# Turning v on VectorE and scaling the attention heads on GpSimd, in an attention and mixture-of-experts layer on one core

## Chip, cores and metric

The kernel runs on one NeuronCore of one Trainium2 chip. The metric is the device time of one execution in microseconds (us). The engines are named as the profile names them: PE (TensorE matmul), PEld (its weight loads), DVE (VectorE), ACT (ScalarE), POOL (GpSimd) and SP (SyncE, which here only issues DMAs). Each engine runs its own instructions in the order in which they were written; they meet through semaphores.

## What is computed

One layer in float32: layer norm, attention with rotary positions, a band mask and a sink column, an output projection and a residual; then layer norm again and a mixture of 8 experts with 2 chosen per token. Cut to what the change touches:

```python
# x: (4, 512, 256); NQ = 32 query heads, NKV = 8 key/value heads, HD = 64
proj = layernorm(x) @ W_qkv
q, k, v = split(proj)
q, k = rope(q), rope(k)
attn = where(mask, -inf, q @ k.T / sqrt(HD))
w = softmax(concat([attn, sink]))[..., :-1]
x = x + (w @ v).reshape(B, L, NQ * HD) @ W_out
x = x + moe(layernorm(x))
```

## The kernel before

**Groups and periods.** The attention part works through 32 groups, 8 key/value heads times 4 batches. A group has one k, one v and four query heads. Its scores come in 16 units of 128x512, two at a time from one PE step. One group's scores take one period; a period has 16 steps, and in each step every engine is given, in this order, work of the group whose scores run (step n of `*_step`), of the next group (n - 16), of the one before (n + 16) and of the one before that (n + 32), and last work of the router. The tables of numbers (`PROJ_PAIR_AT`, `ROT_AT`, `HEADS_AT` and so on) say at which n a piece is written. There is no scheduler: the order on an engine is the order of writing.

**A group's way through the engines.** PE projects k, v and the first two query heads in two halves (`project_pair`, L1508), in steps 0 and 2 of the period before the group's own. ACT copies them out (`chunk_out`, L844) into `chunk_sb`: the tile named KV has k in partitions 0 to 63 and v in 64 to 127; Q01 and Q23 hold two query heads each. For the rotation, SP moves halves of these tiles into `swap_sb` by DMA (`swap_halves`, L492), and POOL rotates (`rotate`, L691, L692 and L696, three instructions per tile; KV's have 64 partitions). The rotated k is doubled by a DMA (`k_twice`). The first score of a group (L1562, n = 0) waits for the rotated KV and Q01 of its group.

**v.** PE turns v by four transposes into a PSUM bank (`turn_v`, L1526, written ahead of the last third of the probabilities times v), ACT copies it to `v_next` (L852), SP stores it to `v_rows` in DRAM (L505) and reads it back four times into `v_quads` (L513), for four 32-row quadrants.

**Probabilities and heads.** DVE takes each unit's scores out of PSUM with the mask and the row maximum (L1162), ACT takes the exponent (L862), DVE turns two units at a time in 32x32 blocks (L1171). In the next period PE multiplies them with v into four PSUM banks `PV` (L1586: 80, 80 and 96 instructions in steps 4, 6 and 8). The denominators go POOL (`sink_arg` L709, `denom` L719), DVE (reciprocal L1180, transpose L1184, after the second unit of the next group), then SP: to DRAM (L521) and back, spread over all partitions, into `recip_wide` (L529). DVE scales the four banks into `heads_sb` (L1191) in step 9. PE projects the heads (L1618, steps 12 and 14), ACT copies the result out (L869, L872, L876), and POOL adds it to the residual (L726, two instructions).

**POOL's and SP's order in a period.** POOL: split of the next weights (L648, L657), rotate Q23, rotate KV, rotate Q01 (step 5), the two residual additions (step 6); with steps 15 and 16 of the group, `sink_arg` and `denom`. In some periods of batches 1 to 3, DMAs with a scatter index are issued from POOL for the router (L774), two of them in step 9. SP: `recip_out`, `recip_spread`, the KV swaps, the Q01 swaps, `k_twice`, three loads of weights, the store and the four loads of v, the Q23 swaps.

Of the kernel before, what the change touches and what calls it, by code (L numbers as in the profile page):

```python
# [20 lines left out]
F32 = mybir.dt.float32  # L21
# [5 lines left out]
P = 128  # L27
# [3 lines left out]
TPB = L // P  # L31
# [28 lines left out]
def moe_layer(nc, x, w_qkv, w_out, sink, gate_w, w1, b1, w2, b2, rope, out):  # L60
    ctx = ExitStack()
    with ctx:
        slot_rows = nc.dram_tensor("slot_rows", (E * CAP, ROW), F32, kind="Internal").ap()

        v_rows = nc.dram_tensor("v_rows", (P, TPB * HD), F32, kind="Internal").ap()
# [111 lines left out]
        s_v_next = sem("s_v_next")  # L177
# [8 lines left out]
        s_heads = sem("s_heads")  # L186
        s_y = sem("s_y")
# [73 lines left out]
        v_next = sb("v_next", [P, TPB, HD], c=actx)  # L261
        qk_st.append(sb("qk_st1", [P, PAIRS + 1, L], c=actx))
        v_quads = [sb(f"v_quads{i}", [P, TPB, TPB * HD], c=actx) for i in range(2)]
# [13 lines left out]
        xn1 = v_next[:, :, :].rearrange("p t d -> p (t d)")  # L277
# [63 lines left out]
        TURN_V_AT, V_NEXT_AT = -8, -7  # L341
        ROT_AT = {2: Q23, -12: KV, -11: Q01}
# [9 lines left out]
        Y_FIRST_OUT_AT, Y_OUT_AT, RESIDUAL_AT = 30, 31, 38  # L352
        ODD_ORDER = (1, 0)
# [85 lines left out]
        def turned_v_bank(g):  # L439

            return PV[0] if g == 0 else PROJ

# [24 lines left out]
        def _(sp):  # L467
# [32 lines left out]
            def v_out(g):  # L500

                sp.wait_ge(s_v_next, g + 1)
                if g > 0:
                    sp.wait_ge(s_v_in[(g - 1) % 2], ((g - 1) // 2 + 1) * (16 * QUADS))
                sp.dma_start(v_rows, v_next[:, :, :].rearrange("p t d -> p (t d)")).then_inc(s_v_out, 16)  # L505

            def v_in(g, j):

                sp.wait_ge(s_v_out, g * 16 + 16)
# [114 lines left out]
        def _(pool):  # L624
# [75 lines left out]
            def pool_step(n, g, j):  # L700
# [19 lines left out]
                if n == RESIDUAL_AT and g < GROUPS - 1:  # L720
                    for i, odd in enumerate(ODD_ORDER):
                        pool.wait_ge(s_y_out, 2 * g + i + 1)
                        if later(2 * g + i):
                            pool.wait_ge(s_residual, 2 * g + i)
                        t = (g // NKV) * TPB + odd
                        nc.gpsimd.tensor_tensor(x_sb[:, t:t + 3:2, :], x_sb[:, t:t + 3:2, :], y_sb[odd][:, :, :],  # L726
                                                ALU.add).then_inc(s_residual, 1)
# [92 lines left out]
        def _(act):  # L820
# [16 lines left out]
            def chunk_out(g, c):  # L837
# [4 lines left out]
                if c == Q23 and g > 0:  # L842
                    act.wait_ge(s_v_turned, g + 1)
# [4 lines left out]
            def v_copy(g):  # L848
                act.wait_ge(s_v_turned, g + 1)
                if g > 0:  # L850
                    act.wait_ge(s_v_out, g * 16)
                nc.scalar.activation(v_next[:, :, :], turned_v_bank(g)[:, 0:TPB * HD].rearrange("p (c d) -> p c d", d=HD),  # L852
                                     ACT.Copy).then_inc(s_v_next, 1)

            def act_step(n, g, j):
                if n in CHUNK_OUT_AT:
                    chunk_out(g, CHUNK_OUT_AT[n])
                if n == V_NEXT_AT:
                    v_copy(g)
                if 0 <= n < UNITS:  # L860
# [3 lines left out]
                                         accum_out=sums[j][:, n:n + 1]).then_inc(s_probs, 1)  # L864
                if n == Y_FIRST_OUT_AT and g < GROUPS - 1:
# [50 lines left out]
            v_copy(0)  # L916
# [44 lines left out]
            def act_ahead(m):  # L961
# [28 lines left out]
                if m in LATE_NORM_AT:  # L990
                    i = LATE_NORM_AT[m]
                    act.wait_ge(s_late, 1 if i < TPB else 2)
                    act.wait_ge(s_v_out, (LATE_PERIODS[i] + 1) * 16)
                    nc.scalar.activation(xn1, x_sb[:, TPB + i, :], ACT.Identity,
# [111 lines left out]
        def _(dve):  # L1106
# [49 lines left out]

            def dve_step(n, g, j):
# [27 lines left out]
                if n == HEADS_AT:  # L1185
                    dve.wait_ge(s_pv, g + 1 + 1)
                    dve.wait_ge(s_recip_in, g * 32 + 32)
                    if later(2 * g):
                        dve.wait_ge(s_y, 2 * g + 1)
# [186 lines left out]
            rotate_q()  # L1376
            dve.wait_ge(s_mask, 1)
# [87 lines left out]
        def _(pe):  # L1465
# [16 lines left out]
            def project(g, j, c):  # L1482
# [4 lines left out]
                else:  # L1487
                    pe.wait_ge(s_v_next, g + 1)
# [25 lines left out]

            def turn_v(g):
                pe.wait_ge(s_chunk_out, g * CHUNKS + (Q01 if g > 0 else KV) + 1)
                if g % NKV == 3 and g > NKV:
                    pe.wait_ge(s_x2T, 2 * (g // NKV))
                if g % NKV == 4 and g > NKV:
                    pe.wait_ge(s_centred, g // NKV)  # L1520
                if g % NKV == 5 and g > NKV:
                    pe.wait_ge(s_place, g // NKV)
                if g - 1 in LATE_PERIODS:
                    pe.wait_ge(s_xT_lo, TPB + LATE_PERIODS.index(g - 1) + 1)
# [23 lines left out]
            def pe_step(n, g, j):  # L1548
# [15 lines left out]
                if n in PV_AT:  # L1564
# [16 lines left out]
                    for blk in PV_AT[n]:  # L1581
                        c, d = divmod(blk, TPB)
                        for a in range(QUADS):
                            rows = slice(a * BLK, (a + 1) * BLK)
                            for p in range(PAIRS):
                                ins = nc.tensor.matmul(PV[a][p * HD:(p + 1) * HD, 0:2 * P],  # L1586
                                                       v_quads[j][rows, d, c * HD:(c + 1) * HD],
# [38 lines left out]
                if n == TURN_V_AT:  # L1626
                    turn_v(g)
# [173 lines left out]
```

## Time and profile before

| | |
|---|---|
| median of 3 runs | 1054.57 us (1053.58 to 1058.2) |
| the profiled execution | 1057.24 us, of which its span is 1055.5 us |
| mean granted TensorE clock, share of full speed | 0.993 |
| busy, share of the span | PE 97%, DVE 88%, POOL 63%, ACT 62% |
| DMA | 112.10 MB in 155893 packets |
| chain that ended last, by engine | PE 56%, DVE 37%, issue 3% |
| chain, largest lines | PE L1586 22%, DVE L1162 16%, DVE L1171 14%, PE L1562 10%, DVE L1191 4% |

Times inside the trace are counted from the first instruction. The attention part ends at about 800 us and the experts follow. The chain of work that ended last is followed back from the last instruction, at each step to what released it. An engine's idle time is given with what released the instruction after it; "issue" there means that nothing which the profile shows was waited for.

### The profile page before, as it was taken

To read this page: it belongs to the slowest core of one execution; us is meant where nothing else is said; L and a number is where in the kernel's file an instruction comes from. 1 tells how busy PE (TensorE), PEld (TensorE's weight loads), DVE (VectorE), ACT (ScalarE), POOL (GpSimd) and SP (SyncE) were. 2 spreads that over 40 slices of the span, in tenths; PEclk is the share of its full clock that TensorE was granted. 3 is DMA by queue.
4 is the path that set the end of the run, shared out by engine and by line. 5 is a ranking of instruction groups with operands and counts; after the bars stand their busy time and mean duration, and the time that the engine had idled before them with its cause. 6 is when DMAs were issued, how large, how long until landed. Compare 5 with 4: busy or idle time off the path is not lost.

```text
span 1055.5 us, 32277 instructions
## 1 busy us (share of the span) xinstructions
PE 1024.9 (97%) x12943; PEld 720.9 (68%) x12943; DVE 926.8 (88%) x1967; ACT 655.0 (62%) x1671; POOL 665.1 (63%) x607
## 2 busy tenths in 40 slices
PE   7899999999999999999999999999988999999996
PEld 4466666666666666666666666666656999999995
DVE  6999999999999999999999999999985787777773
ACT  4666667666667766667776666776663555445551
POOL 6667776777666888666787777777752333333332
PEclk9999999999999999999999999999989999999998
DMA  3534544544333334333334334333424555555521
GB/s 112 142 108 118 137 131 140 132 112 135 93 83 83 96 99 111 99 104 81 80 95 114 100 103 121 98 83 96 119 70 162 119 119 123 117 123 124 101 46 21
DMA packets 155893, 112.10 MB, mean 106 GB/s; under 512 B 76480, under 2 KB 145152, under 8 KB 155616
## 3 DMA queue, kind: packets, MB, share of 16 engines
q1 hardware_dynamic: 137680, 90.03, 33.0%
q0 software_dynamic: 7296, 8.55, 4.8%
q10 hardware_dynamic: 10768, 11.46, 3.6%
q8 instruction: 102, 1.67, 0.7%
q14 instruction: 47, 0.39, 0.1%
HBM read 74.84 MB, written 21.83 MB: 92 GB/s over the span
## 4 chain that ended last, share of the span: by engine, by line
PE 56%; DVE 37%; issue 3%; ACT 1%; POOL 1%; DMA 1%; SPq 0%; POOLq 0%; DVEq 0%; ACTq 0%
PE bank L1586 22%; DVE probs_ring L1162 16%; DVE probs_t L1171 14%; PE bank L1562 10%; PE bank L1739 9%; PE bank L1750 6%; DVE heads_sb L1191 4%; PE bank L1753 3%; PE bank L1618 1%; PE bank L1508 1%; PE bank L1526 1%; PE bank L1533 1%; DVE neg_max L1162 0%; ACT probs_ring L862 0%; PE bank L1491 0%
## 5 line engine op out<-in xcount | busy, mean ns | idle before, releaser
L862 ACT ACTIVATE probs_ring<-probs_ring,neg_max 128x512 f32<-128x512 f32 x512 | 365.8, 717 | 210.3 <-DVE neg_max L1162 209.6
L1162 DVE CUSTOM_DVE_ANT_0 probs_ring<-bank,mask,sink_neg 128x512 f32<-128x512 f32 x512 | 360.1, 737 | 26.6 <-PE bank L1562 25.5
L1171 DVE STREAM_TRANSPOSE probs_t<-probs_ring 128x1024 f32<-128x1024 f32 x256 | 317.5, 1240 | 0.2 <-ACT probs_ring L862 0.2
L1562 PE MATMUL bank<-qk_st 64*128 64x512 f32 x1024 | 281.1, 625 | 11.9 <-DVE neg_max L1162 7.4
L1586 PE MATMUL bank<-probs_t,v_quads 32*64 32x256 f32 x8192 | 247.6, 381 | 0.1
L1586 PEld LDWEIGHTS bank<-probs_t,v_quads 32*64 32x64 f32 x8192 | 179.1, 132 | 76.5 <-issue 48.8
L691 POOL TENSOR_TENSOR chunk_sb<-chunk_sb,rope_sb 128x512 f32<-128x512 f32 (+1 forms) x94 | 120.0, 1276 | 103.9 <-issue 82.7
L810 POOL DMA_INDIRECT out<-expert_sb,slots x40 | 78.8, 1969 | 143.1 <-DVE expert_sb L1428 134.5
L1562 PEld LDWEIGHTS bank<-qk_st 64*128 64x128 f32 x1024 | 85.3, 186 | 77.4 <-DVE neg_max L1162 41.8
L696 POOL TENSOR_TENSOR qk_st<-chunk_sb,swap_sb 128x512 f32<-128x512 f32 (+1 forms) x94 | 120.2, 1279 | 7.4
L1618 PEld LDWEIGHTS bank<-wo_sb,heads_sb 64*128 64x128 f32 x992 | 96.1, 187 | 37.4 <-issue 29.2
L692 POOL TENSOR_TENSOR swap_sb<-swap_sb,rope_sb 128x512 f32<-128x512 f32 (+1 forms) x94 | 120.5, 1281 | 0.0
L1077 ACT ACTIVATE hidden<-bank,b_sb 128x320 f32<-128x320 f32 x128 | 60.6, 525 | 95.7 <-PE bank L1739 95.7
L1618 PE MATMUL bank<-wo_sb,heads_sb 64*128 64x256 f32 x992 | 117.4, 376 | 0.0
L1750 PE MATMUL bank<-w_part,hidden_hi 128*128 128x512 f32 x320 | 114.1, 398 | 0.0
L1508 PE MATMUL bank<-xcur,w_hi 64*128 64x512 f32 x496 | 100.9, 481 | 0.0
L862 ACT ACTIVATION_READ_ACCUMULATOR probs_ring<-probs_ring,neg_max 128x1 f32 x512 | 97.4, 190 | 0.0
L1753 PE MATMUL bank<-w_part,hidden_lo 128*128 128x256 f32 x320 | 90.1, 282 | 0.0
L726 POOL TENSOR_TENSOR x_sb<-x_sb,y_sb 128x512 f32<-128x512 f32 x62 | 79.2, 1277 | 4.5
L1739 PE MATMUL bank<-slots_hi,w_hi 128*128 128x320 f32 x256 | 79.5, 310 | 0.5 <-DVE expert_sb L1428 0.5
L1739 PE MATMUL bank<-slots_lo,w_hi 128*128 128x320 f32 x256 | 79.0, 308 | 0.0
L1739 PE MATMUL bank<-slots_hi,w_lo 128*128 128x320 f32 x256 | 79.0, 308 | 0.0
(191 smaller groups left out, 1342.7 us busy)
## 6 DMA issues: line engine op xcount, KB each, us to landing
v_quads<-v_rows SPq DMA_DIRECT2D x128, 128.0 KB
recip_wide<-recip_rows SPq DMA_DIRECT2D x64, 256.0 KB
w_raw<-in_L_ffn_w SPq DMA_DIRECT2D x14, 1024.0 KB, 7.6
swap_sb<-chunk_sb SPq DMA_DIRECT2D x314, 32.0 KB
w_raw<-in_L_attn_W_qkv SPq DMA_DIRECT2D x32, 256.0 KB, 2.9
slot_rows<-x2T ACTq DMA_DIRECT2D x8, 662.5 KB, 5.8
slots_cut<-slot_rows SPq DMA_DIRECT2D x56, 80.0 KB, 3.0
w_raw<-in_L_attn_W_qkv SPq DMA_DIRECT2D x64, 64.0 KB, 2.7
```

The source lines that it names most:

```text
L691: nc.gpsimd.tensor_tensor(straight, straight, rope_sb[rows, 0, :], ALU.mult).then_inc(s_pool, 1)
L692: nc.gpsimd.tensor_tensor(swapped, swapped, rope_sb[rows, 1, :], ALU.mult).then_inc(s_pool, 1)
L696: nc.gpsimd.tensor_tensor(qk_st[j][rows, PAIRS if c == KV else c - Q01, :], straight, swapped, ALU.add).then_inc(s_rot, 1)
L862: nc.scalar.activation(probs[(g * UNITS + n) % RING][:, :], probs[(g * UNITS + n) % RING][:, :], ACT.Exp, bias=neg_max[j][:, n:n + 1], sca ...
L1162: nc.vector.tensor_tensor_reduce(probs[(g * UNITS + n) % RING][:, :], SCORE[SCORE_OF[n // 2][n % 2]][:, :], mask[:, L - P - t * P:2 * L - ...
L1171: nc.vector.transpose(probs_t[j][:, :, (h // 2) * (2 * P):(h // 2 + 1) * (2 * P)] .rearrange("p b (h q) -> p h b q", h=2)[:, :, :, t * BLK ...
L1562: nc.tensor.matmul(SCORE[SCORE_OF[n // 2][hh]][:, :], qk_st[j][half, h // 2, t * P:(t + 1) * P], qk_st[j][half, PAIRS, :], start=True, sto ...
L1586: ins = nc.tensor.matmul(PV[a][p * HD:(p + 1) * HD, 0:2 * P], v_quads[j][rows, d, c * HD:(c + 1) * HD], probs_t[j][rows, blk, p * 2 * P:(p ...
L1618: ins = nc.tensor.matmul(PV[a][:, 0:D], heads_sb[rows, a, h * P:(h + 1) * P], wo_sb[rows, (g % NKV) * 2 + h, :], start=(half == 0 and h == ...
L1739: ins = nc.tensor.matmul(banks[4 + 2 * (c % 2) + half][:, 0:HALF], w[:, kc, c * P:(c + 1) * P], a[:, at:at + HALF], start=(kc == 0 and m = ...
L1750: nc.tensor.matmul(FFN2[s][:, :], hidden_hi[:, c, s * P:(s + 1) * P], w2_parts[e % 2][:, c, :, :].rearrange("p t d -> p (t d)"), start=(c ...
L1753: ins = nc.tensor.matmul(FFN2[s][:, 0:D], hidden_lo[:, c, s * P:(s + 1) * P], w2_hi[e % 2][:, c, :], start=False, stop=(c == HC - 1))
```

## The change

v is no longer turned by PE. DVE turns it with one transpose in 32x32 blocks (`turn_v`, step 9, where the scaling of the heads was), out of the KV tile into partitions 64 to 127 of the KV swap tile, which were free. The ACT copy to `v_next` is gone. SP stores the turned v with two DMAs whose runs are 128 B (before: one DMA with runs of 1 KB), and reads it back with runs of 4 KB (before: 1 KB). PE's waits that stood in `turn_v` move to the projection of Q23 (L1491), which follows two steps later.

The heads of all groups but the last are copied out of `PV` by ACT (four 128x256 copies, step 9) and scaled in place by POOL (two 128x512 multiplications, step 9), each half with a semaphore of its own; the output projection waits for the first half, and inside its first step for the second. The last group keeps DVE's scaling.

The late layer norms of later batches, which shared a buffer with `v_next`, get one of their own (`xn1`) and wait for PE's turning of the tile before instead of the store of v.

POOL's order changes: the rotation of Q01 moves from step 5 to step 10, behind the heads; the two residual additions move from one place in step 6 to steps 4 and 9.

```diff
-        TURN_V_AT, V_NEXT_AT = -8, -7
-        ROT_AT = {2: Q23, -12: KV, -11: Q01}
+        TURN_V_AT = -7
+        ROT_AT = {2: Q23, -12: KV, -6: Q01}
...
-        Y_FIRST_OUT_AT, Y_OUT_AT, RESIDUAL_AT = 30, 31, 38
-        ODD_ORDER = (1, 0)
+        Y_FIRST_OUT_AT, Y_OUT_AT = 30, 31
+        RESIDUAL_AT = {36: 1, 41: 0}
...
             def v_out(g):
-                sp.wait_ge(s_v_next, g + 1)
+                sp.wait_ge(s_v_turned, g + 1)
...
-                sp.dma_start(v_rows, v_next[:, :, :].rearrange("p t d -> p (t d)")).then_inc(s_v_out, 16)
+                for q in range(HD // BLK):
+                    sp.dma_start(v_rows.rearrange("j (b d) -> j b d", d=HD)[:, :, q * BLK:(q + 1) * BLK],
+                                 v_turned[q * BLK:(q + 1) * BLK, :].rearrange("j (b i) -> j b i", i=BLK)
+                                 ).then_inc(s_v_out, 16)
...
                 for a in range(QUADS):
-                    sp.dma_start(v_quads[j][a * BLK:(a + 1) * BLK, :, :],
-                                 v_rows.rearrange("(c j) n -> j c n", j=BLK)).then_inc(s_v_in[j], 16)
+                    sp.dma_start(v_quads[j][a * BLK:(a + 1) * BLK, :, :].rearrange("j b d -> j (b d)"),
+                                 v_rows).then_inc(s_v_in[j], 16)
...
+                if n == HEADS_AT and g < GROUPS - 1:
+                    pool.wait_ge(s_recip_in, g * 32 + 32)
+                    for half in range(2):
+                        part = slice(2 * half, 2 * half + 2)
+                        pool.wait_ge(s_heads_raw, 2 * g + half + 1)
+                        nc.gpsimd.tensor_tensor(heads_sb[:, part, :], heads_sb[:, part, :], recip_wide[:, part, :],
+                                                ALU.mult).then_inc(s_heads, 1)
...
+                if n == HEADS_AT and g < GROUPS - 1:
+                    act.wait_ge(s_pv, g + 1 + 1)
+                    if later(2 * g):
+                        act.wait_ge(s_y, 2 * g + 1)
+                    for a in range(QUADS):
+                        ins = nc.scalar.activation(heads_sb[:, a, :], PV[a][:, 0:2 * P], ACT.Copy)
+                        if a % 2 == 1:
+                            ins.then_inc(s_heads_raw, 1)
...
+            def turn_v(g):
+                dve.wait_ge(s_chunk_out, g * CHUNKS + KV + 1)
+                if g > 0:
+                    dve.wait_ge(s_v_out, g * 32)
+                nc.vector.transpose(v_turned, chunk_sb[KV][HD:P, :]).then_inc(s_v_turned, 1)
...
-                if n == HEADS_AT:
+                if n == TURN_V_AT and g > 0:
+                    turn_v(g)
+                if n == HEADS_AT and g == GROUPS - 1:
...
-                for c in range(TPB):
-                    ins = nc.tensor.transpose(turned_v_bank(g)[:, c * HD:(c + 1) * HD],
-                                              chunk_sb[KV][HD:P, c * P:(c + 1) * P],
-                                              identity[HD:P, HD:P])
-                ins.then_inc(s_v_turned, 1)
...
-                    pe.wait_ge(s_heads, 2 * g + (half if g == GROUPS - 1 else 1) + 1 + 1)
+                    pe.wait_ge(s_heads, 2 * g + half + 1 + 1)
...
+                            if half == 0 and second == 1:
+                                pe.wait_ge(s_heads, 2 * g + 1 + 1 + 1)
```

On POOL, in the period of group 13, one of those with two scatter DMAs in step 9, before: the last five rows of the rotations, the residual, the DMAs, and `sink_arg` and `denom` of the group.

```order
L691 TENSOR_TENSOR chunk_sb<-chunk_sb,rope_sb 64x512
L692 TENSOR_TENSOR swap_sb<-swap_sb,rope_sb 64x512
L696 TENSOR_TENSOR qk_st<-chunk_sb,swap_sb 64x512
L691 TENSOR_TENSOR chunk_sb<-chunk_sb,rope_sb 128x512
L692 TENSOR_TENSOR swap_sb<-swap_sb,rope_sb 128x512
L696 TENSOR_TENSOR qk_st<-chunk_sb,swap_sb 128x512
L726 TENSOR_TENSOR x_sb<-x_sb,y_sb 128x2x256 x2
L774 DMA slot_rows<-xn,scatter_idx 5120x265 x2
L709 TENSOR_TENSOR sink_arg<-neg_max,sink_neg 128x16
L719 TENSOR_TENSOR denom<-sums,sink_exp 128x16
```

The same place after; line numbers have moved by a few (L690, L691, L695 are the rotation, L733 the residual, L724 the heads, L781 the scatter).

```order
L690 TENSOR_TENSOR chunk_sb<-chunk_sb,rope_sb 64x512
L691 TENSOR_TENSOR swap_sb<-swap_sb,rope_sb 64x512
L695 TENSOR_TENSOR qk_st<-chunk_sb,swap_sb 64x512
L733 TENSOR_TENSOR x_sb<-x_sb,y_sb 128x2x256
L724 TENSOR_TENSOR heads_sb<-heads_sb,recip_wide 128x512 x2
L733 TENSOR_TENSOR x_sb<-x_sb,y_sb 128x2x256
L781 DMA slot_rows<-xn,scatter_idx 5120x265 x2
L690 TENSOR_TENSOR chunk_sb<-chunk_sb,rope_sb 128x512
L691 TENSOR_TENSOR swap_sb<-swap_sb,rope_sb 128x512
L695 TENSOR_TENSOR qk_st<-chunk_sb,swap_sb 128x512
L708 TENSOR_TENSOR sink_arg<-neg_max,sink_neg 128x16
L718 TENSOR_TENSOR denom<-sums,sink_exp 128x16
```

Between the rotation of KV (64 partitions) and that of Q01 (128) now stand a residual addition, both heads, the other residual addition and the scatter DMAs.

On DVE, around step 9 of a period in the middle of the attention part, before:

```order
L1171 STREAM_TRANSPOSE probs_t<-probs_ring 128x2x16x32
L1191 TENSOR_TENSOR heads_sb<-bank,recip_wide 128x256 x4
L1162 ISA probs_ring,neg_max<-bank,mask,sink_neg 128x512
L1162 ISA neg_max 128x1
L1162 ISA probs_ring,neg_max<-bank,mask,sink_neg 128x512
```

and after (L1174 takes the scores out, L1183 turns the probabilities):

```order
L1183 STREAM_TRANSPOSE probs_t<-probs_ring 128x2x16x32
L1167 STREAM_TRANSPOSE swap_sb<-chunk_sb 64x512
L1174 ISA probs_ring,neg_max<-bank,mask,sink_neg 128x512
L1174 ISA neg_max 128x1
L1174 ISA probs_ring,neg_max<-bank,mask,sink_neg 128x512
```

The four scaling instructions, which wait for the probabilities times v, give way to one transpose, which waits for the copied KV tile and for the store of the turned v of the group before.

## Rows read from the trace of the kernel before

**Rows 1.** Page, part 1: busy us (share of the span) xinstructions.

```profile
PE 1024.9 (97%) x12943; PEld 720.9 (68%) x12943; DVE 926.8 (88%) x1967; ACT 655.0 (62%) x1671; POOL 665.1 (63%) x607
```

**Rows 2.** DVE in time order: start us, us, what [idle before <-releaser].

```profile
417.44 1.42 DVE L1191 TENSOR_TENSOR heads_sb<-bank,recip_wide 128x256 f32<-128x256 f32 x4 [0.51 <-PE bank L1586]
418.78 0.74 DVE L1162 CUSTOM_DVE_ANT_0 probs_ring<-bank,mask,sink_neg 128x512 f32<-128x512 f32 x1
```

**Rows 3.** PE in time order, one period, first score to the next one's.

```profile
401.28 1.02 PE L1562 MATMUL bank<-qk_st 64*128 64x512 f32 x4
...
414.15 0.40 PE L1526 MATMUL bank<-identity,chunk_sb 64*128 64x64 f32 x4
414.49 2.85 PE L1586 MATMUL bank<-probs_t,v_quads 32*64 32x256 f32 x96
417.26 1.13 PE L1562 MATMUL bank<-qk_st 64*128 64x512 f32 x4
...
425.19 1.02 PE L1562 MATMUL bank<-qk_st 64*128 64x512 f32 x4
```

**Rows 4.** POOL in order of time, the same period.

```profile
412.83 1.27 POOL L691 TENSOR_TENSOR chunk_sb<-chunk_sb,rope_sb 64x512 f32<-64x512 f32 x1 [2.36 <-issue]
...
419.25 1.29 POOL L696 TENSOR_TENSOR qk_st<-chunk_sb,swap_sb 128x512 f32<-128x512 f32 x1
420.49 2.71 POOL L726 TENSOR_TENSOR x_sb<-x_sb,y_sb 128x512 f32<-128x512 f32 x2
```

**Rows 5.** Groups by line: xcount | busy us, mean ns | idle before.

```profile
L726 POOL TENSOR_TENSOR x_sb<-x_sb,y_sb 128x512 f32<-128x512 f32 x62 | 79.2, 1277 | 4.5
L691 POOL TENSOR_TENSOR chunk_sb<-chunk_sb,rope_sb 64x512 f32<-64x512 f32 x31 | 39.4, 1272 | 88.1 <-issue 82.7 <-DMA swap_sb<-chunk_sb 5.2
L774 POOL DMA_INDIRECT slot_rows<-xn,scatter_idx x32 | 32.4, 1013 | 39.4 <-DMA swap_sb<-chunk_sb 16.5 <-DVE xn L403 11.8 <-issue 6.0
L876 ACT ACTIVATE y_sb<-bank 128x256 f32<-128x256 f32 x62 | 20.2, 382 | 0.0
L1448 DVE STREAM_TRANSPOSE slots_t<-slots_cut 128x1280 f32<-128x1280 f32 x7 | 10.5, 1507 | 1.7 <-DMA slots_cut<-slot_rows 1.7
```

**Rows 6.** SP's issues in order of time, the period of rows 3.

```profile
406.79 1.29 SPq L529 DMA_DIRECT2D recip_wide<-recip_rows  x2
408.13 4.42 SPq L492 DMA_DIRECT2D swap_sb<-chunk_sb  x6
```

**Rows 7.** PE in time order: first scores of groups 1, 30 and 31.

```profile
41.07 1.09 PE L1562 MATMUL bank<-qk_st 64*128 64x512 f32 x3 [1.05 <-DVE neg_max L1162]
...
739.37 1.02 PE L1562 MATMUL bank<-qk_st 64*128 64x512 f32 x4
...
762.90 1.02 PE L1562 MATMUL bank<-qk_st 64*128 64x512 f32 x4
```

**Rows 8.** POOL in time order: KV's rotation begins, periods of groups 1 and 30.

```profile
54.96 1.28 POOL L691 TENSOR_TENSOR chunk_sb<-chunk_sb,rope_sb 64x512 f32<-64x512 f32 x1 [5.36 <-issue]
...
752.13 1.27 POOL L691 TENSOR_TENSOR chunk_sb<-chunk_sb,rope_sb 64x512 f32<-64x512 f32 x1
```

**Rows 9.** POOL in order of time: the second scatter DMA of a pair.

```profile
354.22 1.01 POOL L774 DMA_INDIRECT slot_rows<-xn,scatter_idx  x1 [0.30 <-issue]
```

**Rows 10.** POOL in order of time, period of group 31.

```profile
780.58 4.56 POOL L780 TENSOR_TENSOR w_lo<-w_raw,w_hi 128x2048 fp32r<-128x2048 f32 x1
789.12 0.22 POOL L709 TENSOR_TENSOR sink_arg<-neg_max,sink_neg 128x16 f32<-128x16 f32 x1 [3.98 <-DVE neg_max L1162]
```

**Rows 11.** A stretch: us, busy PE PEld DVE ACT POOL, clock, DMA, GB/s.

```profile
766.80:770.20 3.40, 2.58 (x20) 0.92 (x28) 3.06 (x7) 3.40 (x10) 2.72 (x3) 0.50 0.11 28
```

**Rows 12.** PE in order of time: scores in that stretch.

```profile
767.62 2.08 PE L1562 MATMUL bank<-qk_st 64*128 64x512 f32 x4 [1.72 <-DVE neg_max L1162]
```

**Rows 13.** DMA issues by line: xcount, KB each, median us from issue to landing.

```profile
slots_cut<-slot_rows SPq DMA_DIRECT2D x56, 80.0 KB, 3.0
v_rows<-v_next SPq DMA_DIRECT2D x32, 128.0 KB, 2.5
```

More of the change, by code:

```diff
@@ L260, in moe_layer @@
         y_sb = [sb(f"y_sb{i}", [P, 2, D], c=actx) for i in range(2)]
-        v_next = sb("v_next", [P, TPB, HD], c=actx)
+        xn1 = sb("xn1", [P, D], c=actx)
         qk_st.append(sb("qk_st1", [P, PAIRS + 1, L], c=actx))
-        v_quads = [sb(f"v_quads{i}", [P, TPB, TPB * HD], c=actx) for i in range(2)]
+        v_quads = [sb(f"v_quads{i}", [P, BLOCKS, HD], c=actx) for i in range(2)]
         probs_ring = sb("probs_ring", [P, RING, L], c=actx)
@@ L719, in pool_step @@
                     nc.gpsimd.tensor_tensor(denom[:, :], sums[j][:, :], sink_exp[:, :], ALU.add).then_inc(s_denom, 1)
[L720 to L727, printed above, removed]
+                if n == HEADS_AT and g < GROUPS - 1:
[5 more added lines that the diff above has]
+                                                ALU.mult).then_inc(s_heads, 1)
+                if n in RESIDUAL_AT and g < GROUPS - 1:
+                    odd = RESIDUAL_AT[n]
+                    i = 1 - odd
+                    pool.wait_ge(s_y_out, 2 * g + i + 1)
+                    if later(2 * g + i):
+                        pool.wait_ge(s_residual, 2 * g + i)
+                    t = (g // NKV) * TPB + odd
+                    nc.gpsimd.tensor_tensor(x_sb[:, t:t + 3:2, :], x_sb[:, t:t + 3:2, :], y_sb[odd][:, :, :],
+                                            ALU.add).then_inc(s_residual, 1)
             roots = [0]
@@ L841, in chunk_out @@
                     act.wait_ge(s_rot, q - CHUNKS + 1)
-                if c == Q23 and g > 0:
-                    act.wait_ge(s_v_turned, g + 1)
+                if c == KV and g > 0:
+                    act.wait_ge(s_v_turned, g)
                 nc.scalar.activation(chunk_sb[c][:, :].rearrange("p (c a i) -> p a c i", a=QUADS, i=BLK),
@@ L915, in _ @@
             chunk_out(0, Q23)
-            v_copy(0)
             def load_x(b):
@@ L992, in act_ahead @@
                     act.wait_ge(s_late, 1 if i < TPB else 2)
-                    act.wait_ge(s_v_out, (LATE_PERIODS[i] + 1) * 16)
-                    nc.scalar.activation(xn1, x_sb[:, TPB + i, :], ACT.Identity,
+                    if i > 0:
+                        act.wait_ge(s_norm_turned, TPB + i)
+                    nc.scalar.activation(xn1[:, :], x_sb[:, TPB + i, :], ACT.Identity,
                                          bias=bias_late[:, i:i + 1], scale=rstd_late[:, i:i + 1]).then_inc(s_norm, 1)
@@ L1376, in _ @@
             rotate_q()
+            turn_v(0)
             dve.wait_ge(s_mask, 1)
@@ L1487, in project @@
                 else:
-                    pe.wait_ge(s_v_next, g + 1)
+                    pe.wait_ge(s_chunk_out, g * CHUNKS + Q01 + 1)
+                    if g % NKV == 3 and g > NKV:
+                        pe.wait_ge(s_x2T, 2 * (g // NKV))
+                    if g % NKV == 4 and g > NKV:
+                        pe.wait_ge(s_centred, g // NKV)
+                    if g % NKV == 5 and g > NKV:
+                        pe.wait_ge(s_place, g // NKV)
+                    if g - 1 in LATE_PERIODS:
+                        pe.wait_ge(s_xT_lo, TPB + LATE_PERIODS.index(g - 1) + 1)
                 for kc in range(KC):
@@ L1639, in _ @@
             ins.then_inc(s_gate_cols, 1)
-            turn_v(0)
             SLOT_PIECES = [(0, 0, 4), (0, 4, 5), (1, 0, 3), (1, 3, 5)]
```

37 lines of the change are left out of this document (6 added, 31 removed).

## The prediction

> **What bounds the kernel now.** I read the engines' busy times first [rows 1]: PE 97% and DVE 88% leave little room, POOL stands at 63% and looks free. Then the chain of work that ended last: 56% PE and 37% DVE, hardly anything of POOL or DMA. In one period of the attention part the two take turns. PE runs the last third of the probabilities times v until 414.49 + 2.85 = 417.34 us [rows 3]; DVE sat idle 0.51 us for it and then scaled the heads in 1.42 us, and only at 418.78 did it take the next scores out of PSUM [rows 2], whose matmuls had been issued at 417.26 [rows 3]. So both things that the change takes off, PE's transposes and DVE's scaling, lie on the path that sets the end today.
>
> A 63% that is an average says nothing of when POOL must be done. PE may not issue the first score of a group before POOL has rotated its KV and Q01. In the period shown, POOL sat idle 2.36 us, began with KV at 412.83, and ended with Q01 at 419.25 + 1.29 = 420.54 [rows 4], 4.65 us before that score at 425.19 [rows 3]. POOL could not begin earlier: KV's group has 88.1 us of idle time before 31 instructions [rows 5], and what the code waits for there are the KV swaps, which SP issues behind the spread of the reciprocals [rows 6]. These wait in turn for the first scores of the running group. **KV's rotation therefore hangs on the first score of its period**, 412.83 - 401.28 = 11.55 us behind it here [rows 3, 4]. Over the periods of groups 1 to 30 (30 such pairs) the distance averages 12.34 us; the first is 54.96 - 41.07 = 13.89, the last 752.13 - 739.37 = 12.76 [rows 7, 8]. The mean period is (762.90 - 41.07) / 30 = 24.06 us [rows 7].
>
> **What goes from PE and DVE.** The next scores were issued at 417.26 and such a pair takes 1.13 us [rows 3]; without PE's transposes in front (414.15 to 414.49, 0.34 us) they are ready at about 418.05, and DVE, with no scaling, could take them then instead of at 418.78 [rows 2]. That is 0.7 us a period. DVE's new transpose stands before it and hides in the wait: it moves 64x512, and the nearest row, 128x1280, takes 1.51 us [rows 5]; nothing to 1.51 us bounds it, and by the columns I take 0.6. Left to themselves, PE and DVE would need about 24.06 - 0.7 = 23.4 us a period.
>
> **What comes to ACT.** Four 128x256 copies out of PSUM, nearest row 0.38 us each [rows 5], one of that size less. The first half is there at most 0.76 us after PE's last product, about 16.5 us into the period. POOL is then still at work on the residual, so ACT's copies cost nothing; if POOL were early, they would be its wait.
>
> **What comes to POOL, on the path.** Between KV's and Q01's rotation now stand four instructions of 128x512: a residual addition, two halves of the heads, a residual addition. The nearest rows are the residual's: 1.28 us each in the group [rows 5], 2.71 for two where the second waits for the first [rows 4]. POOL starts the next one slightly before the last has ended (420.49 against 420.54), so I take 1.24 each, 4.95 in all; the ends are 4.8 and 5.4. The two rotations last 420.54 - 412.83 = 7.71 us [rows 4]. From a group's first score to the next one's the path now is: 12.34 to KV's rotation, 7.71 for the two rotations, 4.95 between them, and some 0.07 for the semaphore (estimate from the gaps between engines in rows 2 and 3), **25.07 us**. This is a loop: the score that it delays is the one from which the next period's swaps are counted, so no slack takes it up. Against 24.06 that is 1.01 us, and over 30 periods **+30.3 us**. The 0.7 us saved on PE and DVE turn into a pause before the first score.
>
> **Scatter DMAs.** A pair of them in step 9 stood behind both rotations; it now stands ahead of Q01's. One takes 1.01 us [rows 5], with 0.30 us between the two [rows 9]: 2.3 us for a pair. Eight periods that also rotate a Q01 have a pair (three each for two batches, two for the last): 8 x 2.3 = **+18.4 us**; the bounds are 8 x 2.0 and 8 x 2.6.
>
> **TensorE's clock.** At the end of the attention part PE paused for 1.72 us [rows 12] and the granted clock stood at 0.50, its lower level of 1.2 GHz [rows 11]; a pair of scores then took 2.08 us [rows 12] against 1.13 [rows 3]. In the eight scatter periods PE would wait 25.07 + 2.3 - 23.4 = 4 us before the first score, so I count one fall of the clock each. The loop hangs on the first score alone, so one costs 2.08 - 1.13 = 0.95 us: 8 x 0.95 = **+7.6 us**.
>
> **The end of the attention part.** In group 31's period POOL turned from a 4.56 us weight split at 785.14 to `sink_arg` at 789.12, with 3.98 us to spare [rows 10]. The heads (2.5 us, not before about 782), a residual (1.24), a scatter pair (2.3) and the split (4.56) now come one after the other and end at 792.6, some 3.4 us too late for `sink_arg`; part of that is hidden by PE's last products. I take **+2 us**, between 0 and 3.4.
>
> **The v path on SP.** One store becomes two, with runs of 128 B, ahead of the Q23 swaps and of the reciprocals. Nearest rows: loads in 128 B runs, 80 KB, land after 3.0 us, the old store after 2.5 [rows 13]. That is 0.5 to 1 us with the second issue, and SP stands idle about that long before the next reciprocal; I take nothing. The Trainium skill, in "DMA: Bandwidth & Descriptors", section "Why small descriptors are slow (HBM only)", says that a fixed cost per packet makes short runs to DRAM slow. By it the store could land later still; the rows show 3.0 against 2.5 us, so the trace agrees only mildly, and what it would do is rival D.
>
> **Edits with no price.** PE's waits that stood in `turn_v` now stand before Q23's projection, two steps later, for events of the same or an earlier step. ACT's copy of the next KV tile waits for DVE's transpose of a period ago. The one turn of v on DVE ahead of group 0 falls into its wait for the first scores. If one of these covers were gone, it would cost the transpose once, 0.6 us.
>
> **The sum.** 30.3 + 18.4 + 7.6 + 2 = 58.3 us, on the profiled execution's 1057.24 us: 1115.5. That execution lies 2.7 us above the median of 1054.57, so the forecast is **1113 us**.
>
> **Rivals.**
> - A, faster. POOL's new order fits into the period after all and PE and DVE keep what they save: 30 x 0.7 = 21 us, 1054.6 - 21 = 1034. For it: POOL is idle over a third of the time [rows 1]. It decides where KV's rotation begins earlier than 23.4 - 7.71 - 4.95 - 0.07 = 10.7 us after the first score; the mean is 12.34 and even the period of rows 3 has 11.55. Chance 0.09.
> - B, the loop closes only just. With the 11.55 us of rows 3 and 4 everywhere it is 24.28 us, 0.22 above 24.06; 30 x 0.22 = 7 us, and with the pairs 1080. The part of it without the pairs would read as no change (1062 and less). Chances 0.10 above 1060 and 0.04 for no change.
> - C, the clock falls in most periods. The pause before the first score is 25.07 - 23.4 = 1.7 us on average, as long as the one beside the fall in rows 12. Then 22 more periods pay 0.95: +21, 1134. Against it: that pause had a shorter one just ahead of it. The Trainium skill, "TensorE: Matmul & The Clock Gate", section "HAM oscillation", tells of loops in which each wait between bursts throttles the array anew; by that rule every period pays. Rows 11 and 12 agree that a pause lowers the clock; none shows a pause in each period. Chance 0.17.
> - D, the store of v lands so late that reciprocals and swaps slip: at 0.5 us a period 15 us more, 1128, chance 0.07.
>
> **How the numbers follow.** The forecast, with its bounds (the four POOL instructions 4.8 to 5.4, the pairs, the clock, the end), has 0.53. Slower by over 0.5% (about what a measurement of this kernel can tell from no change): 0.53 + 0.10 + 0.17 + 0.07 = 0.87; within it 0.04; faster 0.09. The range goes from B's 1080 to a little above C, 1140; outside it are A, no change, and some 0.05 of C and D beyond the top.
>
> **What would show it.** Right: PE idle before most first scores, released by POOL's rotation; no idle time on POOL between KV's rotation and `sink_arg`; first scores 25 us apart and 27 or more in scatter periods; the granted clock at 0.50 after those. DVE no longer waits for L1586. Wrong: Q01's rotation ends before PE has finished the group (A), or KV's rotation begins within 10.7 us of the first score.

## The result, and the profile after

| | before | after |
|---|---|---|
| median | 1055.25 us (5 runs, 1053.58 to 1058.2) | 1122.81 us (5 runs, 1119.36 to 1124.67) |
| ratio, 95% interval | | 1.063 (1.060 to 1.067) |
| the profiled execution, its span | 1057.24, 1055.5 us | 1119.37, 1117.6 us |
| mean granted clock | 0.993 | 0.976 |

The changed kernel is 6.3% slower; the forecast was 1113 us, in a range from 1080 to 1140. Part 1 of the page of after (busy us, share of the span, instructions) is to be read beside [rows 1]: POOL has taken on 75 us, and PE, with 128 instructions fewer, is busy for a smaller share of a longer span.

```profile
PE 1038.3 (93%) x12815; PEld 713.2 (64%) x12815; DVE 917.9 (82%) x1875; ACT 687.7 (62%) x1763; POOL 740.2 (66%) x669
```

Of the groups by line, the first is PE's scores (last column: idle time ahead of them, and who ended it). No score waited for POOL before; now those of 30 groups do, for the last instruction of Q01's rotation, and POOL's share is still only 66%. The other three are POOL's heads, residual additions and first instruction of KV's rotation.

```profile
L1568 PE MATMUL bank<-qk_st 64*128 64x512 f32 x1024 | 290.9, 645 | 55.1 <-POOL qk_st L695 44.5
...
L724 POOL TENSOR_TENSOR heads_sb<-heads_sb,recip_wide 128x512 f32<-128x512 f32 x62 | 78.4, 1284 | 12.7 <-ACT heads_sb L868 12.6
L733 POOL TENSOR_TENSOR x_sb<-x_sb,y_sb 128x512 f32<-128x512 f32 x62 | 78.9, 1272 | 0.2
L690 POOL TENSOR_TENSOR chunk_sb<-chunk_sb,rope_sb 64x512 f32<-64x512 f32 x31 | 39.4, 1272 | 107.2 <-issue 99.8 <-DMA swap_sb<-chunk_sb 7.3
```

POOL in order of time, the period of group 17 (start us, us, instruction, idle time before it), the counterpart of [rows 4]:

```profile
462.83 1.26 POOL L690 TENSOR_TENSOR chunk_sb<-chunk_sb,rope_sb 64x512 f32<-64x512 f32 x1 [4.47 <-issue]
...
466.64 1.25 POOL L733 TENSOR_TENSOR x_sb<-x_sb,y_sb 128x512 f32<-128x512 f32 x1
467.86 2.53 POOL L724 TENSOR_TENSOR heads_sb<-heads_sb,recip_wide 128x512 f32<-128x512 f32 x2
470.36 1.26 POOL L733 TENSOR_TENSOR x_sb<-x_sb,y_sb 128x512 f32<-128x512 f32 x1
471.59 1.27 POOL L690 TENSOR_TENSOR chunk_sb<-chunk_sb,rope_sb 128x512 f32<-128x512 f32 x1
...
474.17 1.28 POOL L695 TENSOR_TENSOR qk_st<-chunk_sb,swap_sb 128x512 f32<-128x512 f32 x1
```

PE in order of time, the first scores of groups 17 and 18, the counterpart of [rows 3, 7]:

```profile
450.99 1.13 PE L1568 MATMUL bank<-qk_st 64*128 64x512 f32 x4 [0.54 <-POOL qk_st L695]
...
475.50 1.13 PE L1568 MATMUL bank<-qk_st 64*128 64x512 f32 x4 [0.58 <-POOL qk_st L695]
```

From the first score to KV's rotation 462.83 - 450.99 = 11.84 us, then POOL without a gap to 474.17 + 1.28 = 475.45, and 0.05 us later the next score. That is the loop of the prediction: its distance averages 12.29 us over groups 1 to 30, where the kernel before had 12.34. The loop isn't POOL's alone in every period: in 14 of the 30, POOL waits 0.1 to 1.8 us for ACT's copies ahead of the heads, 7.4 us in all, and these copies wait for PE's products (of the 12.6 us in the row of the heads above, the other 5.3 belong to group 31's period).

The period of group 14 has a scatter pair. POOL, then PE, then a stretch of the clock (us, busy PE PEld DVE ACT POOL, clock, DMA, GB/s), the counterpart of [rows 9, 11, 12]:

```profile
387.83 1.28 POOL L733 TENSOR_TENSOR x_sb<-x_sb,y_sb 128x512 f32<-128x512 f32 x1
389.25 1.01 POOL L781 DMA_INDIRECT slot_rows<-xn,scatter_idx  x1
390.56 0.97 POOL L781 DMA_INDIRECT slot_rows<-xn,scatter_idx  x1 [0.30 <-issue]
391.56 1.29 POOL L690 TENSOR_TENSOR chunk_sb<-chunk_sb,rope_sb 128x512 f32<-128x512 f32 x1
```

```profile
395.46 1.76 PE L1568 MATMUL bank<-qk_st 64*128 64x512 f32 x4 [3.01 <-POOL qk_st L695]
```

```profile
395.90:399.20 3.30, 3.30 (x16) 2.11 (x14) 1.96 (x5) 1.91 (x6) 3.16 (x4) 0.50 0.00 0
```

The pair keeps Q01's rotation back by 391.56 - 389.11 = 2.45 us, PE pauses for 3.01, and the granted clock stands at 0.50, its lower level of 1.2 GHz, right behind.

**Where the 62 us of span are.** The 30 periods of groups 1 to 30 take (818.25 - 42.28) us, 25.87 each against 24.06: +54.1. The 22 without a pair ahead of Q01 average 25.03, the eight with one 28.16. The period of group 0 takes 24.15 us instead of 22.19: +2.0. From group 31's first score to the end it is 1117.6 - 818.25 = 299.4 us against 1055.5 - 762.90 = 292.6: +6.8. The start is 0.8 shorter. The sum is 62.1.

### The profile page after: what moved, and what is told of

Its sections match the earlier page's. It is cut to its first block and busy times, and to the rows that moved or that the text cites. A ratio compares the mean times of both kernels' runs of the same rounds, so it can differ in the third digit from the quotient of the medians.

```text
span 1117.6 us, 32144 instructions
## 1 busy us (share of the span) xinstructions
PE 1038.3 (93%) x12815; PEld 713.2 (64%) x12815; DVE 917.9 (82%) x1875; ACT 687.7 (62%) x1763; POOL 740.2 (66%) x669
## 5 line engine op out<-in xcount | busy, mean ns | idle before, releaser
L1174 DVE CUSTOM_DVE_ANT_0 probs_ring<-bank,mask,sink_neg 128x512 f32<-128x512 f32 x512 | 362.6, 742 | 101.4 <-PE bank L1568 98.3
L1568 PE MATMUL bank<-qk_st 64*128 64x512 f32 x1024 | 290.9, 645 | 55.1 <-POOL qk_st L695 44.5
L1183 DVE STREAM_TRANSPOSE probs_t<-probs_ring 128x1024 f32<-128x1024 f32 x256 | 317.3, 1239 | 0.4 <-ACT probs_ring L860 0.2
L690 POOL TENSOR_TENSOR chunk_sb<-chunk_sb,rope_sb 128x512 f32<-128x512 f32 (+1 forms) x94 | 120.4, 1281 | 124.5 <-issue 99.8
L695 POOL TENSOR_TENSOR qk_st<-chunk_sb,swap_sb 128x512 f32<-128x512 f32 (+1 forms) x94 | 120.0, 1276 | 7.4
L691 POOL TENSOR_TENSOR swap_sb<-swap_sb,rope_sb 128x512 f32<-128x512 f32 (+1 forms) x94 | 120.1, 1277 | 0.0
L1530 PE MATMUL bank<-xcur,w_hi 64*128 64x512 f32 x496 | 110.6, 522 | 0.0
L724 POOL TENSOR_TENSOR heads_sb<-heads_sb,recip_wide 128x512 f32<-128x512 f32 x62 | 78.4, 1284 | 12.7 <-ACT heads_sb L868 12.6
L851 ACT ACTIVATE chunk_sb<-bank 128x512 f32<-128x512 f32 x94 | 55.0, 585 | 51.0 <-PE bank L1530 51.0
L1742 PE MATMUL bank<-slots_hi,w_hi 128*128 128x320 f32 x256 | 79.5, 310 | 0.1
L733 POOL TENSOR_TENSOR x_sb<-x_sb,y_sb 128x512 f32<-128x512 f32 x62 | 78.9, 1272 | 0.2
```

Of the source, the lines that this page charges most:

```text
L690: nc.gpsimd.tensor_tensor(straight, straight, rope_sb[rows, 0, :], ALU.mult).then_inc(s_pool, 1)
L691: nc.gpsimd.tensor_tensor(swapped, swapped, rope_sb[rows, 1, :], ALU.mult).then_inc(s_pool, 1)
L695: nc.gpsimd.tensor_tensor(qk_st[j][rows, PAIRS if c == KV else c - Q01, :], straight, swapped, ALU.add).then_inc(s_rot, 1)
L1174: nc.vector.tensor_tensor_reduce(probs[(g * UNITS + n) % RING][:, :], SCORE[SCORE_OF[n // 2][n % 2]][:, :], mask[:, L - P - t * P:2 * L - ...
L1183: nc.vector.transpose(probs_t[j][:, :, (h // 2) * (2 * P):(h // 2 + 1) * (2 * P)] .rearrange("p b (h q) -> p h b q", h=2)[:, :, :, t * BLK ...
L1568: nc.tensor.matmul(SCORE[SCORE_OF[n // 2][hh]][:, :], qk_st[j][half, h // 2, t * P:(t + 1) * P], qk_st[j][half, PAIRS, :], start=True, sto ...
```

## The experiments

Theory: POOL's chain from KV's rotation to the next first score sets the period; what is put on it costs its full length, what stands beside it costs nothing. Rivals: POOL's load as such, the traffic of the scatters, or the new v path.

**One product more on POOL, in two places.** It writes a tile that the rotation overwrites. The second place is step 3 (`n == -13`), ahead of KV's rotation; there the product also waits for the scores of the group two before.

```
+ if n == -6 and g > 0:            # between heads and Q01's rotation
+     nc.gpsimd.tensor_tensor(qk_st[j][:, 0, :], rope_sb[:, 0, :], rope_sb[:, 1, :], ALU.mult)
```

> The changed kernel with one more 128x512 product on POOL in each period, right ahead of Q01's rotation (its result is overwritten). Theory (POOL's chain): all of its 1.24 us reach the next first score, 30 x 1.24 = 37 us, and the longer pauses may lower the clock more often: 1155 to 1175 us. Rival (POOL has slack there): less than 10 us over the changed kernel.

> The same added product, once in each period, but ahead of KV's rotation, where POOL waits 3.5 us on average for the swaps. Theory (only what stands behind KV's rotation counts): 0 to 8 us over the changed kernel: 1119 to 1131 us. Rival (POOL's load as such is what costs): as much as in the place ahead of Q01, some 37 us.

Measured: 1170.62 us between (1.107 of before, 1.103 to 1.111) and 1122.69 us ahead (1.061, 1.058 to 1.065); the changed kernel has 1122.81. The groups by line show the same 1282 ns in both (the first row is the one between, the other two are the run with the product ahead of KV): ahead of KV most of it is paid out of POOL's idle time there, 79.5 us where the changed kernel had 107.2.

```profile
L701 POOL TENSOR_TENSOR qk_st<-rope_sb 128x512 f32<-128x512 f32 x31 | 39.7, 1282 | 0.1
```

```profile
L690 POOL TENSOR_TENSOR chunk_sb<-chunk_sb,rope_sb 64x512 f32<-64x512 f32 x31 | 39.4, 1272 | 79.5 <-issue 72.9 <-DMA swap_sb<-chunk_sb 6.4
L702 POOL TENSOR_TENSOR qk_st<-rope_sb 128x512 f32<-128x512 f32 x30 | 38.5, 1282 | 0.0
```

So place, not load: the same 1.3 us a period cost 48 us in the one place and nothing that the runs can show in the other. The 48 are more than 30 x 1.24 = 37, and most of the rest goes with the clock. With the product between, PE paused 0.5 to 2.6 us in the 22 normal periods, and the clock stood at 0.50 behind five of these pauses, as in this one (PE, then the stretch):

```profile
531.65 1.86 PE L1570 MATMUL bank<-qk_st 64*128 64x512 f32 x4 [1.88 <-POOL qk_st L695]
```

```profile
532.00:535.30 3.30, 3.30 (x14) 2.01 (x12) 1.76 (x5) 1.81 (x7) 3.07 (x4) 0.50 0.00 0
```

**The two terms one at a time, and together.**

```
- SCATTER_AT = {89: (0, 1), 99: (2,), 105: (3, 4), 115: (5,), 121: (6, 7)}
+ SCATTER_AT = {90: (0, 1), 99: (2,), 106: (3, 4), 115: (5,), 122: (6, 7)}   # e1, e3
- RESIDUAL_AT = {36: 1, 41: 0}
+ RESIDUAL_AT = {35: 1, 36: 0}                                               # e2, e3
```

> The changed kernel, with the scatter pairs of step 9 moved one step on, behind the rotation of Q01. Theory (POOL's chain from KV's rotation to the next first score sets the period): the eight periods with a pair lose the 2.45 to 2.7 us that a pair takes there, about 20 us, and with their pauses of 3 us or more most of the falls of the clock, some 5 us more: 1095 to 1103 us against 1119 to 1124; periods with a pair come down from 27.2-29.4 us to 25-26.5. Rival (the scatter's traffic, not its place on POOL, lengthens these periods): within 5 us of the changed kernel.

> The changed kernel, with both residual additions off the stretch between the heads and the rotation of Q01: the first stands ahead of KV's rotation, where POOL has 3.5 us of idle time on average, the second in the gap between KV's rotation and the heads. Theory (POOL's chain): one 128x512 instruction of 1.24 us less between KV's rotation and the next first score, up to 30 x 1.24 = 37 us; PE and the copies on ACT keep some of it, since the heads cannot start before PE's products: 1085 to 1100 us. Rival (PE or ACT sets the period through the heads, POOL only follows): less than 8 us.

> The changed kernel with both edits: scatter pairs behind Q01's rotation, residual additions ahead of the heads. Theory (POOL's chain): the gains add, and PE becomes the bound at 23.5 to 24.2 us a period: 1052 to 1075 us. Rival (something else in the change costs, the v path or the copies on ACT): more than 1085 us.

Measured: 1097.09, 1087.67 and 1064.47 us (1.038, 1.030 and 1.008 of before). The scatter pairs are worth 25.7 us (the prediction had 18.4 + 7.6 = 26.0 for them and their clock), one residual addition 35.1 us (30 x 1.24 = 37), both together 58.3, nearly their sum. (The second edit moves both residual additions, but one of them still stands behind KV's rotation, so one is taken off the loop.) In the run with the scatter pairs moved, the clock never stood at 0.50 between 24 and 826 us. The rivals, the scatters' traffic and PE or ACT through the heads, fall.

**The turn of v alone.** The changed kernel with the heads scaled on DVE as before, Q01's rotation at -11 and the residual additions at 38 and 39.

> Of the change only the turn of v on VectorE, with its two stores; the heads are scaled on VectorE, and POOL has the order of the kernel before. Theory: PE's 0.34 us a period go, DVE's 0.7 us transpose lies in its wait for PE ahead of the heads but for 0.2 us: 1045 to 1065 us, near the kernel before. Rival (the two stores with 128 B runs let reciprocals and swaps slip by 0.5 us a period and more): 1070 us and more.

Measured: 1065.87 us (1.009, 1.006 to 1.012), a little above the upper end. Of the 30 periods the median is 0.2 us longer than before: the turn (0.71 us) stands right ahead of the heads on DVE, which now wait for PE twice only, 27 times in the kernel before (19.1 us in all there; DVE's waits: us in total, times, longest):

```profile
DVE heads_sb L1190 <- PE bank L1577: 7.7, 2, 7.4
```

The first two periods are longer by 1.0 and 0.7 (seven others by 0.5 to 0.8), with the spreads of the reciprocals issued 8.2 and 7.3 us after the first score instead of 5.5 to 6.0. The turn of v is thus worth 10 of the changed kernel's 68 us at most.

**Both new operations with POOL's order eased.** As in the run with both edits, but both residual additions ahead of KV's rotation, and the losses at both ends mended:

```
- RESIDUAL_AT = {36: 1, 41: 0}
+ RESIDUAL_AT = {34: 1, 35: 0}
- SPLIT_AT, SECOND_SPLIT_AT = -15, -10
+ SPLIT_AT, SECOND_SPLIT_AT = -15, -5
+ LAST_SCATTER_AT = {90: (0, 1), 99: (2,), 106: (3, 4), 115: (5,), 120: (6, 7)}   # for the last batch that scatters
```

> The changed kernel with its two new operations kept and POOL's order eased: both residual additions ahead of KV's rotation, scatter pairs behind Q01's (for the last of them, in the period of group 31, ahead of the heads), the second weight split behind Q01's rotation again. Theory (POOL's chain): the path from KV's rotation to the next first score is then two rotations and the heads, 12.4 + 7.7 + 2.5 + 0.07 = 22.7 us, so PE sets the period; the periods of the run with both edits in which PE did not wait for POOL were 0.13 to 0.84 us shorter than the same ones of the kernel before, 0.36 on average, 30 x 0.36 = 11 us: 1040 to 1052 us, faster than the kernel before. Rival (the copies on ACT and the heads on POOL make Y late, or residuals ahead of KV delay KV): 1056 us or more.

> The order as in the eased kernel and the heads on ACT and POOL, but v still turned by TensorE and copied out by ScalarE as in the kernel before. Theory: PE is the bound there, so its 0.34 us of transposes come back in each period, 10 us over the eased kernel: 1050 to 1062 us. Rival (with DVE freed of the heads the turn of v costs as much on DVE, or its two stores do harm): as fast as the eased kernel or faster.

Measured: 1057.66 us (1.001, 0.999 to 1.004) and 1056.44 us (1.000, 0.999 to 1.002). The loss is gone, both ends with it (group 31's first score to the end 292.2 us, group 0's period 23.1), but the gain did not come. The heads alone landed in their range, but not for the reason given: the turn of v on PE costs no 10 us, and the rival (as fast as the eased kernel) came true. The theory was wrong in both runs.

With the heads alone, PE is the bound at the same period as before. Its first scores of groups 17 and 18 are 23.90 us apart, as are those of the kernel before (425.19 and 449.09):

```profile
425.21 1.02 PE L1579 MATMUL bank<-qk_st 64*128 64x512 f32 x4
...
449.11 1.02 PE L1579 MATMUL bank<-qk_st 64*128 64x512 f32 x4
```

In between PE is busy for 23.84 of the 23.90 us (us, busy PE PEld DVE ACT POOL, clock, DMA, GB/s):

```profile
425.21:449.11 23.90, 23.84 (x359) 15.43 (x357) 21.15 (x44) 16.83 (x49) 19.41 (x18) 1.00 0.33 89
```

With v turned on DVE too, many periods did come down to 23.66, but groups 1, 8 and 10 took 27.53, 26.62 and 25.33 us. SP's issues around the period of group 8, which begins at 212.10, show why (start us, us, what):

```profile
208.08 1.27 SPq L503 DMA_DIRECT2D v_rows<-swap_sb  x2
214.17 1.74 SPq L513 DMA_DIRECT2D v_quads<-v_rows  x4
...
220.97 1.30 SPq L529 DMA_DIRECT2D recip_wide<-recip_rows  x2
```

The loads of v wait on SP for the two stores (`v_rows`) to land, and the spread behind them goes out at 8.87 us instead of 5.5. That is rival D of the prediction: in the changed kernel POOL's chain hid it, and with that chain shortened it became the next thing late.

**The stores of v earlier.** DVE's turn four steps earlier, the stores ahead of the copy of K:

```
- TURN_V_AT = -7
+ TURN_V_AT = -11
  swap_halves(g + 1, Q01)
+ v_out(g + 1)
  k_twice(g + 1, (g + 1) % 2)
...
- v_out(g + 1)
```

> The eased kernel, with DVE's turn of v four steps earlier and its stores ahead of the copy of K and the weight loads on SP, so that the loads of v no longer wait there for the stores to land. In the eased kernel SP came to the reciprocals late in periods 1 to 10 (spread issued at 5.9 to 9.0 us instead of 5.5), and the worst of these periods took 25.3 to 27.5 us. Theory (with POOL's chain shortened, the two stores on SP are the next thing late): these periods fall to 23.4 to 24.0 us and the spreads are issued at 5.5 to 5.6 us again: 1040 to 1050 us, faster than the kernel before. Rival (the periods are long for another reason, such as the first period's late swaps or the residuals ahead of KV): 1054 us or more.

> The turn of v on VectorE alone (heads on VectorE, POOL's order of the kernel before), with the same earlier stores. Theory: the run with the turn of v alone was 9.6 us over the kernel before, of which about 0.2 us a period, 6 us, is DVE's transpose and the rest the late stores: 1058 to 1064 us. Rival (the stores were all of it): 1050 to 1057 us.

> The changed kernel with nothing but the earlier turn and stores of v. Theory: with POOL's chain as the bound, the stores lie beside it and moving them gives nothing: 1116 to 1126 us. Rival (the store of v delays reciprocals and swaps in the changed kernel too): 1105 us or less.

Measured: 1059.81 us on the eased kernel (1.003, 1.001 to 1.005), 1056.16 with the heads on DVE (1.000, 0.998 to 1.002), 1128.34 on the changed kernel (1.067, 1.063 to 1.071): none as expected. SP's lateness was gone, with spreads at 5.5 to 6.0 us in 29 of the 30 periods of the eased kernel, and most of these took 23.3 to 24.2. But groups 13 and 29 took 26.93 and 27.36: the turn now met the routing's small instructions on DVE (group 13's period; the scores that waited last):

```profile
337.12 0.71 DVE L1168 STREAM_TRANSPOSE swap_sb<-chunk_sb 64x512 f32<-64x512 f32 x1
...
342.42 1.04 DVE L404 TENSOR_TENSOR xn<-gates,top_sum 128x32 f32<-128x32 f32 x1
343.39 0.74 DVE L1175 CUSTOM_DVE_ANT_0 probs_ring<-bank,mask,sink_neg 128x512 f32<-128x512 f32 x1
```

With the heads on DVE the early turn takes the 9.7 us of the turn of v back; since it moves the turn and the stores together, it doesn't tell their shares apart, and these stay open; the trace of the run with the turn of v alone speaks for the turn in most periods and for the stores in the first two. On the changed kernel the earlier stores gave nothing, as the theory has it, but the run came out 5.5 us above after, 2 us over the expected end; six of its eight scatter periods are longer (28.48 instead of 27.22 for group 13). That fits the same meeting on DVE; it isn't shown.

**The stores ahead, the turn where it was.** The eased kernel with the move of `v_out` alone:

> The eased kernel with one edit on SP: the two stores of v stand ahead of the copy of K and of the weight loads, while DVE's turn of v stays in its old step. (With the turn four steps earlier, the spreads of the reciprocals were on time in nearly all periods, but the turn met the routing's small operations on DVE in periods 13 and 29, which took 3 us more each.) Theory: the stores land while SP issues the other transfers, no period is held up by SP, and PE sets nearly all of them at 23.3 to 24.5 us; sum of the 30 periods 715 us, 1044 to 1053 us in all. Rival (the copy of K behind the stores is late for the first score, or the first period's DVE and later meetings take the gain): 1056 us or more.

Measured: 1050.17 us, 0.994 of before (0.992 to 0.996). Groups 13 and 29, whose periods were long with the early turn, now take 24.2 and 23.3 us, so the turn's step made them long. First scores of groups 17 and 18, 23.65 us apart:

```profile
423.81 1.02 PE L1569 MATMUL bank<-qk_st 64*128 64x512 f32 x4
...
447.46 1.02 PE L1569 MATMUL bank<-qk_st 64*128 64x512 f32 x4
```

Part 1 of its page: PE back at 97%, with less work than before.

```profile
PE 1017.9 (97%) x12815; PEld 706.8 (67%) x12815; DVE 920.7 (88%) x1875; ACT 681.6 (65%) x1763; POOL 741.2 (71%) x669
```

So with POOL's and SP's orders suited to them, the kernel with the two new operations is some 6 us faster than before, and as ordered in the change it is 68 us slower. What the new orders would do for the old operations was not run, so how much of the 6 us is the operations' own stays open.

## Why the prediction was right, step by step

- **POOL's loop** (25.07 us, +30.3). Right: the 22 periods without a pair ahead of Q01 (the normal ones) average 25.03 us. That it fits to 0.04 us is in part luck: KV's rotation begins 12.16 us after the first score in them, not 12.34, and from there to the end of Q01's rotation it takes 12.81 us, not 7.71 + 4.95 = 12.66, since in ten of them POOL waits for ACT's copies. That wait contradicts "no idle time on POOL between KV's rotation and `sink_arg`" and the copies that cost nothing. The two places of the added product, and the residual addition taken out, show that this is the cause.
- **Scatter pairs and the clock** (18.4 + 7.6 = 26.0 over the normal period). The eight periods lie 28.16 - 25.03 = 3.13 us above the others, 25.0 in all. The split between the two is off: a pair keeps Q01 back by 2.45 to 2.7 us, not 2.3, since the gap ahead of the rotation counts too, and the clock fell after six of the eight pauses, not after all. What a fall costs lies in the period that follows, so that only four of the six are paid within the eight; one falls on group 16, one on group 31.
- **The price of one fall of the clock** (0.95 us, from the first score alone). Too small where it can be read singly. The period of group 16, with no pair but with the clock at 0.50 from 423.13 to 429.96, takes 26.99 us instead of 25.03: its heads begin 19.34 us after the first score, not at 16.6 to 18.4 as in the other normal periods, because PE's products came late (they ended 18.4 us after the first score, in the others at 15.4 to 16.7). Through ACT's copies the heads wait for PE, so the loop does not hang on the first score alone.
- **The end of the attention part** (+2, at most 3.4). It is +6.8: this is the term that was mis-sized, and the reason was wrong. What held PE up was not `sink_arg` but the scatter pair itself, behind the heads on POOL; SP's load of the slots waits for it, and PE for that load (PE, SP and POOL in the period of group 31):

```profile
849.74 0.79 PE L1547 MATMUL bank<-before_r,ones_r 128*128 128x512 f32 x1 [5.43 <-DMA slots<-slot_rows]
```

```profile
845.67 0.34 SPq L601 DMA_DIRECT2D slots<-slot_rows  x1
```

```profile
837.82 2.51 POOL L724 TENSOR_TENSOR heads_sb<-heads_sb,recip_wide 128x512 f32<-128x512 f32 x2 [5.27 <-ACT heads_sb L868]
840.29 1.27 POOL L733 TENSOR_TENSOR x_sb<-x_sb,y_sb 128x512 f32<-128x512 f32 x1
841.71 1.01 POOL L781 DMA_INDIRECT slot_rows<-xn,scatter_idx  x1 [0.15 <-issue]
843.02 0.97 POOL L781 DMA_INDIRECT slot_rows<-xn,scatter_idx  x1 [0.30 <-issue]
```

  SP issued that load 27.4 us after the first score, against 20.0 before (782.87 - 762.90), where PE did not wait for it at all. The prediction counted the pair's time on POOL there, but not who waits for its data. In the run with both edits, where this pair is still behind the heads, the end took 296.8 us; in the eased kernel, with the pair ahead of them, 292.2 again.
- **The first period** was no term of the sum: +2.0. Q01's rotation fell behind the second weight split, and its last instruction released the score (POOL, then PE):

```profile
36.57 1.83 POOL L656 TENSOR_TENSOR w_lo<-w_raw,w_hi 128x768 fp32r<-128x768 f32 x1
38.35 1.27 POOL L690 TENSOR_TENSOR chunk_sb<-chunk_sb,rope_sb 128x512 f32<-128x512 f32 x1
...
40.94 1.26 POOL L695 TENSOR_TENSOR qk_st<-chunk_sb,swap_sb 128x512 f32<-128x512 f32 x1
```

```profile
42.28 1.10 PE L1568 MATMUL bank<-qk_st 64*128 64x512 f32 x3 [1.05 <-POOL qk_st L695]
```

  With the split behind the rotation the period took 23.1, and with the heads alone, v turned on PE, 21.96. That points to the turn of v for the rest: DVE's 0.71 us lie in that period without any heads leaving it.
- **What PE and DVE save** (0.7 us a period, 23.4). Too much: where POOL and SP were out of the way, 30 periods averaged 23.84 us, 0.22 below before, and either half of the change alone, its orders mended, gave nothing (1.000 both times). With the heads alone PE sets the same period as before; that DVE does so with the turn of v alone was not shown. The misjudged saving cost the sum nothing, as POOL's loop lay above both, but rival A's 1034 us was out of reach.
- **DVE's transpose** (0.6): 0.71 us. **The store of v on SP** (0): right for this kernel, since moving it gave nothing: SP issued its loads of v 2.96 us (median) after the first store, 2.52 before. Rival D is there all the same, hidden by POOL's chain. **Rival C** (the clock falls in most periods) did not happen. The pauses that it counted on were 1.7 us; those of the normal periods averaged 0.8 and reached 1.33, without a fall, and with the product between, at 0.5 to 2.6 us, five in 22 fell. The Trainium skill, "TensorE: Matmul & The Clock Gate", section "HAM oscillation", tells of a loop whose waits of 3 to 5 us throttle the array anew in every turn. This trace agrees for the pauses of 3.0 to 3.8 us, and there six times in eight; the prediction carried it over to pauses of about half that length, for which the section makes no such claim.

The forecast lay 10 us under the result. Of these, 4 are the profiled execution's 1119.37 against the sum's 1115.5: both ends, 2.0 + 6.8 us where 2 were counted, less what the loop and the start came out shorter. The other 6 are the distance of profiled execution and median: the one before lies 2.7 us above its median of then, the one after 3.4 us below its own. The sum came so close to the profiled execution because these misses partly cancel.

## What to carry to other kernels

An engine that is busy two thirds of the time can set the period: follow the loop from the event that starts a period to the one that ends it, and add what a change puts on it, wherever the idle time of that engine lies. Before moving an operation onto it, ask what on the loop could stand in the idle part instead; here a few step numbers and one moved line made 73 us of difference with the same operations. And at both ends of a loop, ask who waits for the data of a step that slips, not only how long the step takes.

## What the hardware showed

- Behind a pause of PE the granted clock falls sometimes, not always. Pauses of up to 1.33 us ahead of the first score never brought it to 0.50 (22 normal periods of after); of those of 0.5 to 2.6 us five in 22 did (the run with the product between), of 3.0 to 3.8 us six in eight (the scatter periods of after), of 4.2 to 5.1 us eight in eight (those of the run with the product between).
- Such a fall costs more than the slower instructions right behind it. In the run with the product between, the periods of groups 6, 8, 19 and 28 follow a fall and take 1.3 to 2.0 us more than the same periods of after and the product (1.24 us) together. Fifteen normal periods with no fall ahead of them in either run come out 0.1 us below that sum on average. The pair of scores at the lower clock costs 0.95 us of it [rows 3, 12].
